# A second attention entered with two blocks instead of four, its weight preparation spread over three engines, and three hardware loops written out

## The reference, cut to what matters

```
x = x + tanh(g_xattn[0]) * attention0(layernorm(x), ctx)           # 16 heads of 16
x = x + tanh(g_ffn[0])   * mixture0(layernorm(x))                  # ternary weights: shared expert + best of 8
x = x + tanh(g_xattn[1]) * attention1(media=ctx, latents=layernorm(x))   # 8 heads of 128
x = x + tanh(g_ffn[1])   * mixture1(layernorm(x))                  # top 2 of 8, capacity, shared expert

attention1: xn = ln(media)*g_m + b_m ; l = ln(latents)*g_l + b_l    # layer norms with weights
            q = (l @ Wq + bq) / sqrt(128) ; k, v = concat(xn, l) @ Wkv + bkv
            out = softmax(q k^T) v @ Wo + bo
```

## Time and profile before

| | |
|---|---|
| median of 3 runs | 1070.16 us (1065.31 to 1075.05) |
| the profiled execution's own time | 1069.45 us |
| its span (first to last instruction) | 1067.7 us |
| PE busy | 956.3 us, 90% |
| DVE busy | 768.2 us, 72% |
| ACT busy | 621.9 us, 58% |
| POOL busy | 230.4 us, 22% |
| mean granted TensorE clock | 0.944 of full speed |

### The profile page before, as it was taken

One profiled execution on the slowest core, in us unless ns is written; L12 is line 12 of the kernel. 1 busy time (PEld: TensorE's weight loads), 2 busy tenths in 40 slices (PEclk: granted clock), 3 DMA queues, 4 the chain that ended last, 5 costly groups with the idle time before them and its releaser, 6 DMA issues. The chain is left out here.

```text
span 1067.7 us, 22058 instructions
## 1 busy us (share of the span) xinstructions
PE 956.3 (90%) x7942; PEld 881.4 (83%) x7942; DVE 768.2 (72%) x1919; ACT 621.9 (58%) x1502; POOL 230.4 (22%) x289
## 2 busy tenths in 40 slices
PE   5899997787997789999999999999978999799992
PEld 4788885676776579999999999999968999699992
DVE  7898886674666697887677676766776877466665
ACT  4788885374885555555555555555538444466560
POOL 3443442023001520000000101010000000566642
PEclk9899997688898799999999999999989999899996
DMA  8511110002562300000000000003024000534517
GB/s 272 188 61 60 44 61 2 2 25 69 178 162 69 73 23 20 2 21 1 21 1 21 2 21 1 21 2 99 1 76 123 1 2 1 134 129 138 148 56 266
DMA packets 68121, 69.24 MB, mean 65 GB/s; under 512 B 14512, under 2 KB 59696, under 8 KB 67888
## 3 DMA queue, kind: packets, MB, share of 16 engines
q1 hardware_dynamic: 61520, 52.89, 16.2%
q0 software_dynamic: 5376, 14.69, 4.8%
q10 hardware_dynamic: 1120, 0.27, 0.1%
HBM read 46.07 MB, written 21.76 MB: 64 GB/s over the span
## 5 line engine op out<-in xcount | busy, mean ns | idle before, releaser
L1558 PE MATMUL a_psK<-a_kvThi,a_wk 128*128 128x512 f32 x256 | 97.4, 421 | 4.9 <-issue 2.6
L314 POOL TENSOR_SCALAR t_neg<-t_raw,t_nthr 128x256 bf16<-128x256 f32 (+1 forms) x54 | 60.7, 1139 | 106.4 <-DVE t_nthr L543 100.4
L1617 PE MATMUL a_psY<-a_nwhi,a_uhi 128*128 128x256 f32 x256 | 73.8, 288 | 5.1 <-DVE a_ulo L1790 5.1
L1677 ACT ACTIVATE a_probs<-a_psS,a_softmax 128x256 f32<-128x256 f32 x128 | 59.6, 471 | 29.6 <-DVE a_softmax L1772 29.6
L1667 ACT ACTIVATE a_khi<-a_psK,a_bk 128x512 fp32r<-128x512 f32 x64 | 44.1, 688 | 50.1 <-PE a_psK L1558 49.4
L1689 ACT ACTIVATE a_uhi<-a_psU 128x512 fp32r<-128x512 f32 x64 | 38.3, 598 | 58.8 <-PE a_psU L1598 58.7
L1598 PE MATMUL a_psU<-a_pTlo,a_tokhi 128*128 128x256 f32 x256 | 72.4, 283 | 0.0
L1598 PE MATMUL a_psU<-a_pThi,a_tokhi 128*128 128x256 f32 x256 | 72.4, 283 | 0.0
L1598 PE MATMUL a_psU<-a_pThi,a_toklo 128*128 128x256 f32 x256 | 72.4, 283 | 0.0
L1617 PE MATMUL a_psY<-a_nwlo,a_uhi 128*128 128x256 f32 x256 | 72.3, 282 | 0.0
L1617 PE MATMUL a_psY<-a_nwhi,a_ulo 128*128 128x256 f32 x256 | 72.2, 282 | 0.0
(11 more groups left out here) (394 smaller groups left out, 3203.3 us busy)
## 6 DMA issues: line engine op xcount, KB each, us to landing
t_raw<-in_L_ffn_expert_w SPq DMA_DIRECT2D x16, 512.0 KB, 3.5
f_raw<-in_fc_T SPq DMA_DIRECT2D x16, 512.0 KB
m_results<-a_zeros SPq DMA_DIRECT2D x8, 512.0 KB
m_sorted<-m_zeros SPq DMA_DIRECT2D x1, 2944.0 KB, 12.6
m_n<-m_sorted SPq DMA_DIRECT2D x23, 128.0 KB, 2.4
m_expert_out<-e_y SPq DMA_DIRECT2D x23, 128.0 KB, 2.2
a_rawkv<-in_L_xattn_Wkv SPq DMA_DIRECT2D x8, 256.0 KB, 3.4
m_n<-in_sh_T SPq DMA_DIRECT2D x2, 1024.0 KB, 7.8
```

The lines of the kernel that those rows point to most:

```text
L314: ins = pool.tensor_scalar(neg[:, own], raw[h % NRAW][:, own], nthr[h % 2][:, n:n + 1], None, ALU.is_lt)
L1558: ins = pe.matmul(psK[:].rearrange("p b t -> p (b t)"), wk[x][:, a, h * DH:(h + 1) * DH], kvT[pair % 2][y][:, a, :, :, :].rearrange("p b m ...
L1617: ins = pe.matmul(psY[:, b, :], u[ch % 2][x][:, f, hh * P:(hh + 1) * P], nw[y][:, f, 2 * j + hh, :], start=first, stop=last, skip_group_ch ...
L1677: act.activation(probs[n % 2][:, b, :], psS[n % 2][:, b, :], ACT.Exp, bias=nmax[:, n % NM, b:b + 1], accum_out=sums[:, n % NM, b:b + 1]).t ...
```

## The change

Seven things, in the order of the code.

1. First attention: in step NB, `signs` of the last half, the last context statistics and norm steps 0 to 7 come after `residual` and `heads_out` instead of before; in step NB+1 norm steps 8 to 15 come after `residual`. In step 0 TensorE's `turn_half(0)` comes after `scores(1, 0, ...)`.
2. The front's three hardware loops become written-out code.
3. `load_small` moves from SP at t = 17 to GpSimd at the start of the routed tiles' block.
4. GpSimd's wait for the stores moves from the end of that block into the entry's block, before the first gather. ScalarE computes one spare Exp at the end of the tiles' block.
5. Entry block: READY 4 -> 2, SOON 8 -> 4. VectorE does the context half of `norm` for blocks 0 and 1 first, then scales rawq in place and rounds it; GpSimd computes Wq's low part between gathers 0, 1 and gathers 2, 3; ScalarE keeps Wk's high part. Transposing Wv is interleaved with the products.
6. Unit block: block 1's transposes go into psU[1] and need not wait for block 0's low part; `values_bias` runs two heads at a time, before unit 0 and in units 0 to 2; `lower_product` 2 heads a unit; norms, turns and tokens of the next pair one or two units later.
7. Blocks 2 and 3 are entered in unit 0 with a norm chain of their own in units 0 and 1; blocks 4 to 7 in units 1 to 4, chain in units 5 to 7; blocks 8 to 15 as before.

The changed lines (unchanged ones left out, indentation cut):

```diff
@@ -575,22 +575,25 @@
-if t >= 1 and due(t + 1):
+if t >= 1 and due(t + 1) and t < NB:
-if NB <= t < NB + 2:
-    if t == NB:
-        k.step(dve.bn_stats(c_stats[:, NB - 1, :], ctx_sb[:, NB - 1, :]))
-    for n in range((t - NB) * 8, (t - NB + 1) * 8):
-        k.step(norm_step(dve, n, *both))
+if t == NB + 1:
+    for n in range(8, 16):
+        k.step(norm_step(dve, n, *both))
+if t == NB:
+    signs(t + 1)
+    k.step(dve.bn_stats(c_stats[:, NB - 1, :], ctx_sb[:, NB - 1, :]))
+    for n in range(8):
+        k.step(norm_step(dve, n, *both))
@@ -769,9 +772,11 @@
-if due(t):
+if due(t) and t > 0:
+if t == 0:
+    turn_half(t)
@@ -853,9 +858,11 @@
+    y = [sb(f"e0_y{i}", [P, D], F32, ahead, "right") for i in range(2)]
+    y_out = [sem(f"e0_out{i}", ahead) for i in range(2)]
-                 xg, yg, xin, x_in, EARLY, A, weights, loaded)
-return dict(n_sb=n_sb, prob=prob, pos=pos, yg=yg, weights=weights, loaded=loaded)
+                 xg, yg, xin, x_in, EARLY, A, weights, loaded, y, y_out)
+return dict(n_sb=n_sb, prob=prob, pos=pos, yg=yg, weights=weights, loaded=loaded, NT=NT, y_out=y_out)
@@ -972,7 +979,7 @@
-with pe.Fori(1, PAIRS // 2 - 1) as i:
+for i in range(1, PAIRS // 2 - 1):
@@ -1014,7 +1021,7 @@
-with act.Fori(1, PAIRS // 2) as i:
+for i in range(1, PAIRS // 2):
@@ -1124,7 +1131,7 @@
-with dve.Fori(2, PAIRS // 2) as i:
+for i in range(2, PAIRS // 2):
@@ -1143,14 +1150,13 @@
-y = [sb(f"e0_y{i}", [P, D], F32, c) for i in range(2)]
-names = "turned scaled steps steps2 split up up_out turned2 silu split2 down y_done out0 out1".split()
+names = "turned scaled steps steps2 split up up_out turned2 silu split2 down y_done".split()
-y_out = [s["out0"], s["out1"]]
+spare = sb("e0_spare", [P, 1], F32, c)
@@ -1192,19 +1198,6 @@
-def load_small():
...
@@ -1214,10 +1207,22 @@
-        if t == WEIGHTS_FROM + len(pieces):
-            load_small()
+@block.gpsimd
+def _(pool):
+    NI = A["L1_xattn_Wq"].shape[1]
+    with nc.allow_non_contiguous_dma(reason="a few hundred small parameters"):
+        for dst, src in ((weights["bq"][:], A["L1_xattn_bq"].rearrange("(h p) -> p h", p=P)),
+                         (weights["bk"][:], A["L1_xattn_bkv"][0:NI].rearrange("(h p) -> p h", p=P)),
+                         (weights["bv"][:], A["L1_xattn_bkv"][NI:2 * NI].rearrange("(h p) -> p h", p=P)),
+                         (weights["bo"][:], A["L1_xattn_bo"].partition_broadcast(P)),
+                         (weights["gam"][:, 0, :], A["L1_xattn_gamma_media"].partition_broadcast(P)),
+                         (weights["gam"][:, 1, :], A["L1_xattn_gamma_lat"].partition_broadcast(P)),
+                         (weights["bet"][:, 0, :], A["L1_xattn_beta_media"].partition_broadcast(P)),
+                         (weights["bet"][:, 1, :], A["L1_xattn_beta_lat"].partition_broadcast(P))):
+            pool.dma_start(dst, src).then_inc(loaded["small"], 16)
@@ -1302,6 +1307,7 @@
+act.activation(spare[:], ident[:, 0:1], ACT.Exp)
@@ -1338,11 +1344,6 @@
-@block.gpsimd
-def _(pool):
-    for b in range(2):
-        pool.wait_ge(y_out[b], (NT + 1 - b) // 2 * 16)
@@ -1365,7 +1366,9 @@
-READY, SOON = 4, 8
+READY, SOON = 2, 4
+ENTRIES = [(READY, SOON), (SOON, 2 * SOON), (2 * SOON, NB)]
+NT0, y_out = begun["NT"], begun["y_out"]
@@ -1391,9 +1394,9 @@
+made_nw = sb("a1_made_nw", [P, KD, NH, D], F32, r)
-made_nw = sb("a1_made_nw", [P, KD, NH, D], F32, r)
@@ -1408,14 +1411,18 @@
-for j in range(NH // 2):
+pe.wait_ge(o_in, NH // 2 * 16)
+def turn_values(j):
-pe.wait_ge(o_in, NH // 2 * 16)
+turn_values(0)
+turn_values(1)
@@ -1423,32 +1430,55 @@
+    if h % 2 == 1 and h // 2 + 2 < NH // 2:
+        turn_values(h // 2 + 2)
-act.wait_ge(q_in, NI // D * 16)
-act.activation(flat(wq[0]), flat(rawq[:]), ACT.Copy, scale=scale).then_inc(s["q_hi"], 1)
+def values(j):
+    act.wait_ge(s["v_turned"], j + 1)
+    act.activation(vT[:, 2 * j:2 * j + 2, :], psW[j % 2][:], ACT.Copy).then_inc(s["v_done"], 1)
-for j in range(NH // 2):
-    act.wait_ge(s["v_turned"], j + 1)
-    act.activation(vT[:, 2 * j:2 * j + 2, :], psW[j % 2][:], ACT.Copy).then_inc(s["v_done"], 1)
+values(0)
+values(1)
+    if h % 2 == 1 and h // 2 + 2 < NH // 2:
+        values(h // 2 + 2)
-for i in range(SOON):
+pool.wait_ge(small_in, 128)
+pool.tensor_copy(bvw[:], bv[:].unsqueeze(2).to_broadcast([P, NH, P]))
+for b in range(2):
+    pool.wait_ge(y_out[b], (NT0 + 1 - b) // 2 * 16)
+for i in range(READY):
+    gather(pool, i)
+pool.wait_ge(s["q_hi"], 1)
+pool.tensor_tensor(flat(wq[1]), flat(rawq[:]), flat(wq[0]).bitcast(F32), ALU.subtract)
+for i in range(READY, SOON):
-dve.wait_ge(s["q_hi"], 1)
-dve.scalar_tensor_tensor(out=flat(wq[1]), in0=flat(rawq[:]), scalar=scale, in1=flat(wq[0]).bitcast(F32),
-                         op0=ALU.mult, op1=ALU.subtract)
+dve.wait_ge(small_in, 128)
+for b in range(2):
+    ins = dve.scalar_tensor_tensor(out=centred[:, b, :], in0=ctx_sb[:, b, :], scalar=c_mean[:, b:b + 1],
+                                   in1=gam[:, 0, :], op0=ALU.subtract, op1=ALU.mult)
+ins.then_inc(s["centred"], 1)
+dve.wait_ge(s["centred"], 1)
+for b in range(2):
+    ins = dve.scalar_tensor_tensor(out=kv[b][:, 0, :], in0=centred[:, b, :], scalar=c_rstd[:, b:b + 1],
+                                   in1=bet[:, 0, :], op0=ALU.mult, op1=ALU.add)
+ins.then_inc(s["normed"], 1)
+dve.wait_ge(q_in, NI // D * 16)
+k.step(dve.tensor_scalar(flat(rawq[:]), flat(rawq[:]), scale, None, ALU.mult))
+dve.tensor_copy(flat(wq[0]), flat(rawq[:])).then_inc(s["q_hi"], 1)
@@ -1461,9 +1491,14 @@
-dve.wait_ge(small_in, 128)
-for b in range(2):
-    norm(dve, b, b + 1, s["centred"], s["normed"])
+dve.wait_ge(s["normed"], 1)
+for b in range(READY):
+    dve.scalar_tensor_tensor(out=centred[:, b, :], in0=x_sb[:, b, :], scalar=x_mean[:, b:b + 1],
+                             in1=gam[:, 1, :], op0=ALU.subtract, op1=ALU.mult).then_inc(s["centred"], 1)
+for b in range(READY):
+    dve.wait_ge(s["centred"], b + 2)
+    dve.scalar_tensor_tensor(out=kv[b][:, 1, :], in0=centred[:, b, :], scalar=x_rstd[:, b:b + 1],
+                             in1=bet[:, 1, :], op0=ALU.mult, op1=ALU.add)
@@ -1492,18 +1527,19 @@
-         "m1_in m1_const stats_done chain combined entered links bv_wide n_lo b_done b_sum").split()
+         "m1_in m1_const stats_done chain combined entered links n_lo b_done b_sum").split()
-PER_UNIT = 4
+kv_turning = [psT[:], psU[1][:].rearrange("p k (m t) -> p k m t", m=2)]
+PER_UNIT = 2
-NORM_AT, TURN_AT, TOKENS_AT = {0: 0, 2: 1}, {3: 0, 5: 1}, {4: 0, 6: 1}
+NORM_AT, TURN_AT, TOKENS_AT = {2: 0, 4: 1}, {4: 0, 6: 1}, {5: 0, 7: 1}
@@ -1542,11 +1578,12 @@
-at_least(pe, s["kv_lo"], b)
+if b != 1:
+    at_least(pe, s["kv_lo"], b)
-        ins = pe.transpose(psT[:, a, m, :], kv[b % 2][:, m, a * P:(a + 1) * P], ident[:])
+        ins = pe.transpose(kv_turning[b == 1][:, a, m, :], kv[b % 2][:, m, a * P:(a + 1) * P], ident[:])
@@ -1618,14 +1655,16 @@
-def values_bias():
-    pe.wait_ge(s["bv_wide"], 1)
-    for h in range(NH):
+def values_bias(part):
+    for h in (2 * part, 2 * part + 1):
-    ins.then_inc(s["b_done"], 1)
+    if h == NH - 1:
+        ins.then_inc(s["b_done"], 1)
+values_bias(0)
@@ -1633,8 +1672,8 @@
-if n == LAG_U - 1:
-    values_bias()
+if n < NH // 2 - 1:
+    values_bias(n + 1)
@@ -1652,8 +1691,10 @@
+if b == 2:
+    act.wait_ge(s["n_lo"], NH)
-               psT[:].rearrange("p a m t -> p a (m t)"), ACT.Copy).then_inc(s["kv_hi"], 1)
+               kv_turning[b == 1].rearrange("p a m t -> p a (m t)"), ACT.Copy).then_inc(s["kv_hi"], 1)
@@ -1694,9 +1735,10 @@
-for b in range(2):
-    stage_kv(b)
-    stage_tokens(b)
+stage_kv(0)
+stage_kv(1)
+stage_tokens(0)
+stage_tokens(1)
@@ -1722,7 +1764,6 @@
-pool.tensor_copy(bvw[:], bv[:].unsqueeze(2).to_broadcast([P, NH, P])).then_inc(s["bv_wide"], 1)
@@ -1747,14 +1788,14 @@
-    dve.wait_ge(s["links"], norm_length(0) * (1 if b < SOON else 2))
+    dve.wait_ge(s["links"], norm_length(0) * (1 if b < SOON else 2 if b < 2 * SOON else 3))
-dve.tensor_tensor(lanes(kvT[pair % 2][1][:, :, bb, :, :]), lanes(psT[:]),
+dve.tensor_tensor(lanes(kvT[pair % 2][1][:, :, bb, :, :]), lanes(kv_turning[b == 1]),
@@ -1815,7 +1856,7 @@
-own, done = (slice(READY, SOON), SOON - READY) if part == 0 else (slice(SOON, NB), NB - READY)
+own, done = slice(*ENTRIES[part]), ENTRIES[part][1] - READY
@@ -1875,13 +1916,16 @@
-if 1 <= n < 1 + SOON - READY:
-    enter(READY + n - 1)
-elif SOON <= n < NB:
+if n == 0:
+    for b in range(*ENTRIES[0]):
+        enter(b)
+elif SOON <= n + 3 < 2 * SOON:
+    enter(n + 3)
+elif 2 * SOON <= n < NB:
-for part, begin in enumerate((SOON - READY + 1, NB)):
+for part, (begin, each) in enumerate(((0, 8), (SOON + 1, 5), (NB, 5))):
-        for step in range((n - begin) * 5, min((n - begin + 1) * 5, norm_length(0))):
+        for step in range((n - begin) * each, min((n - begin + 1) * each, norm_length(0))):
```

13 lines of the change are left out of this document (1 added, 12 removed).

## The result

The changed kernel took 1065.21 us, the kernel before 1072.24 (medians of 22 runs each): a ratio of 0.995, 95% interval 0.993 to 0.997. That is 3.5 to 7.3 us less by the ratio's interval; 20.7 were forecast. The profiled execution took 1062.81 us (span 1061.1), 6.6 less than that of before.

The account below looks back on a forecast made before the run. TensorE, busy 90% of the span, bounds the kernel; gains come only where it waits, in four places. Terms -3.3 - 9.1 - 4.5 - 5.8 - 1.4 + 3.4 = -20.7 take 1069.45 to 1049 us, range 1043 to 1060.

Parts of the forecast that it names:

- End of the first attention: Last steps of the first attention: VectorE's reordered stream starts the second reciprocal earlier, 3.3 us gained, bounds 2.3 to 4.9.
- Front written out: Shared expert's front: without loops, two table loads and ScalarE's 5.40 us wait go, 9.1 us gained.
- lower end of 1.9: Front: least gain from writing it out, if only the two table loads go, 1.9 us.
- Rival 1: Front: the unnamed waits are not the loops', so it gains 1.9 to 4 us, total 1055; chance 0.23.
- Small parameters: Routed tiles: moving the loads off SP's queue gains 5.5 us; their meeting other loads costs 1.0.
- rival 2: Routed tiles: small parameters hold up the first tiles' loads, some 6 us instead of 1.0, total 1054; chance 0.10.
- Entry block with the wait for the stores: Second attention's entry: earlier start and work shared among three engines end the block at 355.0, 5.8 us gained.
- Rival 3: Entry block: GpSimd is shut out while VectorE scales and rounds, 1.5 to 2 us more, total 1050.5; chance 0.12.
- Blocks turned: From block 0's first transpose to the first keys: block 1's pass goes behind block 0's, 1.4 us gained.
- Units 0 to 6: Second attention's first units: VectorE's added combines, statistics and norm chain cost 3.4 us, bounds 0 and 5.
- rival 4: Behind the front: unnamed waits of 7.89 us hit new places, making it slower from the third, 1072.5; chance 0.05.
- The rest: From the low keys of unit 7 to the kernel's end: no change forecast, 0.

Follow-up runs that it names:

- e7: Changed kernel with Wq's low part made by VectorE instead of GpSimd; ratio to the kernel before 0.993.
- a_after: The changed kernel, unedited, run and profiled again on another chip; ratio to the kernel before 0.990.
- e15: Changed kernel with 14 of the front's 16 scatters left out and its three hardware loops put back, on a chip with unnamed waits; front 59.3 us.
- e10: Changed kernel with VectorE's old order in the last two steps of the first attention; ratio to the kernel before 0.998.
- a_before: The kernel before, unedited, run and profiled again on another chip, where it took 1054.7 us; front 59.8 us.
- first pair: First measurement and traces of the kernel before and the changed kernel: 1072.24 and 1065.21 us, ratio 0.995.
- e9: Changed kernel with the eight small parameters back on SP's queue at t = 17; ratio to the kernel before 0.999.
- second pair: Both kernels, unedited, run and profiled again on another chip; spans 1054.0 us before and 1049.0 us after, ratio 0.990.
- e4: Changed kernel with 14 of the front's 16 scatters left out and its three hardware loops put back, run once; front 58.9 us.
- e5: Changed kernel with the front's three hardware loops put back; ratio to the kernel before 0.994, front 58.8 us.
- e13: Changed kernel with 14 of the front's 16 scatters left out and its three loops put back, on a chip without unnamed waits; front 59.4 us.
- e8: Changed kernel with twelve scatters to spare DRAM added between the twelve gathers at the units' start; median 1078.5 us, ratio to the kernel before 1.009.
- e11: Changed kernel with Wq's low part on VectorE and the twelve gathers in three groups of four; 1060.5 us, ratio to the kernel before 0.991.
- e16: The edits of e14 to the changed kernel, repeated on a chip with unnamed waits; 1056.4 us, ratio to the kernel before 0.990.
- e14: e11 with the second mixture's first ten gathers in two groups of five, on a chip without unnamed waits; ratio to the kernel before 0.992.

## Why the prediction was wrong, by its steps

- *What bounds the kernel.* Right for the gains: they lie in the four places named. The losses lie outside them, in the first units and behind unit 63.
- *End of the first attention, -3.3.* Right: 3.9 by the middle of the profiles. Part of it doesn't always last: in a_after TensorE's clock was at the lower level for 24 us behind it (194.6 to 218.2), in the changed kernel's first trace for 14 and in e7's for 17.
- *Front written out, -9.1.* The step that failed: "The wait of 5.40 before the second goes if the loop makes it." The loop didn't make it (e15 has the loop and no wait; the changed kernel has 4.03 and 2.03 and e10 5.39 without a loop). The table loads were worth about 1 us: on the chips without the waits both follow waits for TensorE's products (0.96 and 1.81 in a_before). My lower end of 1.9 was too high as well. Measured in the first pair was -3.0, on the second chip +2.7, with the clock against it; on chips with the waits the written-out front took 61.7 to 66.7 us in six profiles. Rival 1 was right in its cause; its 1.9 to 4 holds for the first pair only.
- *Small parameters, -5.5 + 1.0.* Right: -5.7 from the first product to the last in both pairs (-6.5 and -4.7 for the whole stage), 2.2 to 3.2 between e9 and its group. The tiles behind the gap gave 0.8 back, where I took 0.3. The +1.0 for the loads stands for something between 0 and 3.2: rival 2's mechanism shows in about half the profiles as one late product, at about half its price of 6 where it is largest, and up to 2.0 of it is TensorE's wait for m_n.
- *Entry block with the wait for the stores, -5.8.* Measured -1.6. The failed step: "Three engines end within 1.5 us of each other", which took Wq's low part on GpSimd as 5.1 us beside a VectorE that it does not touch. Its own work was sized well (4.4 us once VectorE's instruction had ended), the overlap was not: it stood behind VectorE's for 2.1 and then held a combine of VectorE for 4.3, which is what is missing. Rival 3 named the contention with only one of its two sides, VectorE shutting GpSimd's gathers out; in the changed kernel no gather of the entry took over 1.38 us.
- *Blocks turned, -1.4.* Right: -1.7 and -1.2.
- *Units 0 to 6, +3.4.* Right where no unnamed wait falls in: +1.9 in the second pair, +1.9 to +4.6 and +3.1 in the mean in nine profiles with the one burst. In the first pair +8.4: the burst of twelve, which the change makes of eight and eight, meets the units. It is what rival 4 allowed for, waits at new places, at 7.9 apiece and without a place; the place could have been looked for wherever a burst of GpSimd's grew longer.
- *The rest.* +3.7 in the first pair, +1.7 in the second. TensorE's clock was at the lower level for 10.2 us instead of 6.8 behind unit 63 in both pairs: that is 1.7 us of work, all of the second pair's. The first pair's other 2.0 stay open: it rests on one profile of before on such a chip.

So on a chip without the waits the sum should have been -3.9 - 1 - 4.7 - 1.6 - 1.2 + 3.1 = -9.3, with the spread between profiles in mind; measured were -10 (0.990) and -6 (0.994). In the first pair the stages read -4.9 - 3.0 - 6.5 - 1.6 - 1.7 + 8.4 - 1.0 + 3.7 = -6.6, the difference of the two spans. That the forecast of 1049 lies near what the changed kernel takes on the chips without waits (1044 and 1047) is chance: before takes 1053 to 1055 there. My range's upper end left out that the gain from the front and the gain from the entry could fail together.

The Trainium skill (SBUF — State Buffer, SBUF: two separate sides) says that VectorE and GpSimd contend for one pair of ports; that between a VectorE operation with two SBUF inputs and a GpSimd operation that reads SBUF, whichever starts first holds the pair for its whole instruction; and that the other is blocked fully. The trace agrees in both directions: the combine of 0.49 us took 4.76 beside GpSimd's instruction, and that one got through 2.1 us late, after Wk's low part. Of the two rules at hand I had weighed only the one on GpSimd's descriptors. The Trainium skill's rule on taken branches (Runtime: NRT & Kernel Launch, Instruction fetch mechanics), which I quoted for the loops, speaks of targets outside the two pages at hand, and no run shows where the loops' targets lay. No wait bears it out here (e4, e5, e13, e15: no unnamed wait over 1 us in their fronts).

What stays open: why the first pair and two groups show the waits and three groups don't, with the same bursts on all; and what the stopped engines wait for. That it is their instructions was argued, not shown. The profile does list two queues of instruction transfers (q8 and q14), and in the changed kernel's trace neither moves anything from 340 to 372 us, before, in and behind unit 2's wait; whether these two serve every engine is not known. Shown, by one or two profiles each, is that the waits become more and longer when the burst is doubled (e8) and go when it is cut (e11, e16) or left out (e15). In unit 2 and the second mixture most of the waits end some 2 us after the burst, those of the front about as it ends, and two of e8's three inside it.

## What to carry to other kernels

Before an idle time without a named releaser is counted as a gain, take a second profile of the same kernel, on another chip if there is one: it costs one run and here would have cut the forecast by a third. Look at what GpSimd does meanwhile: the waits stood beside bursts of ten, twelve, sixteen and 24 indirect DMAs, and not beside bursts of eight, five and four. Cutting the longer ones is worth trying where a chip shows the waits; it may cost something where none does (e14). And a long elementwise instruction given to GpSimd "because it is free" can be paid by VectorE's two-input instructions beside it (4.3 us here for work that takes VectorE 2.3); count the overlap before giving it away.

## What the hardware did that I had not expected

- One GpSimd subtraction of 128x2048 (6.51 us) kept a VectorE combine of 0.49 us for 4.76, after waiting 2.1 itself for VectorE's 128x2048 subtraction. Cut in four pieces it kept the two combines for 2.91 and slowed a chain of small instructions from 3.2 to some 4.8.
- Two kinds of chip: before takes 1053 to 1057 us on three, 1069 to 1072 on two and in the first pair. The unnamed waits (front, second mixture) make up most of the difference: 67.0 against 59.8 us in the front, 301.7 against 294.3 after the units.
- In written-out code a wait of 5.39 us (e10) stood where the loop had one of 5.40, at 253.8 and 253.6 us into the span. The loops' own cost was about 1 us.
